# First layer of a two-layer kernel: the state gradient of the block three back right behind the state product, and VectorE's update and bias work put into another order

## The chip, the cores and the metric

The kernel runs on one core of a Trainium2 chip. The time is the device time of one execution in microseconds (us); the time of a kernel is the median of its runs.

## What is computed

Two layers act on x, four sequences of 512 tokens with 128 features. Each layer normalizes x and adds an attention part and an expert part to it. The change concerns the attention part of the first layer, a recurrence over chunks of 64 tokens for 16 heads of width 64, in which each head keeps a 64x64 state W and a bias b, updated by a gradient step for each chunk:

```python
def step(carry, inp):
    W, bb = carry
    xq_c, xk_c, xv_c = inp
    lr = jax.nn.sigmoid(jnp.einsum('bhkc,hcd->bhkd', xk_c, theta) + tb)
    eta = token_eta * (BASE_LR * lr / HD)
    Z1 = xk_c @ W + bb
    mu = Z1.mean(-1, keepdims=True)
    std = jnp.sqrt(Z1.var(-1, keepdims=True) + EPS)
    x_hat = (Z1 - mu) / std
    y = g * x_hat + be
    grad_output = y - (xv_c - xk_c)
    gxh = grad_output * g
    grad_x = (HD * gxh - gxh.sum(-1, keepdims=True) - x_hat * (gxh * x_hat).sum(-1, keepdims=True)) / (HD * std)
    dW = jnp.einsum('bhkc,bhkd->bhcd', eta * xk_c, grad_x)
    db = (eta * grad_x).sum(-2, keepdims=True)
    Wn, bn = (W - dW, bb - db)
    Zq = xq_c @ Wn + bn
    ...
    out = xq_c + g * ((Zq - mu2) / std2) + be
    return ((Wn, bn), out)
```

The first layer's expert part (16 experts that each take 32 tokens of a sequence), the second layer's attention and its four rounds of a mixture of four experts follow; the change does not touch them.

## The kernel before, in words

Each engine has a program of its own, written out by hand, and the programs meet through semaphores. There is no scheduler: the order of the calls in the source is the order in which an engine works, and an engine that waits holds up all that stands behind it.

The recurrence has 8 chunks (NC). A chunk is cut into four blocks, two halves of the heads (hf) by two pairs of sequences (g), so that there are 32 blocks. The loop `for s in range(4 * NC + 6)` stands in the programs of TensorE (PE), VectorE (DVE) and ScalarE (ACT), and one to 4 * NC in that of GpSimd (POOL). Step s does the gradient side of block s and the query side of block s - 4, which reads the state after the update by that block. Below, the class of a step is s mod 4.

A step runs through the engines as follows, with the names of the helpers and the lines of the profile.

- PE: `XK_` turns the keys (L1336). `bias_rows` puts the bias into the two banks of Z (L1283); at an even s it waits for `bias_split`, and always for `xhat` and `normed` of the step before, which still read those banks. `state_q` and `state` multiply queries and keys by the state (L1292); both wait for `state_updated`, the update by block s - 4. `target` (L1324, then L1238 to L1240) multiplies the tokens by the weights of the target. In odd steps `bias` sums the rated gradients of two blocks into the bias bank (L1357). `queries` and `keys` make the features of a coming chunk (L1238 to L1240). `att` multiplies the normed and turned output by the output weights in steps of class 0 and 1 (L1400). `dW` is the state gradient, 16 matmuls of 64x64 (L1372). `turn` turns the normed output of the step before (L1389).
- ACT: squares of Z (`squares`, L485, and `squares_q`, L521), a copy of the target out of its bank (`take_u`, L495), in odd steps the rounded part of the bias (`bias_high`, L516), then the deviation (`deviation`, L490), the copy of the queries (L510) and `deviation_q` (L526).
- DVE: `centre` of the block before (L830), the two sums of squares (L792, L854), the reciprocal (L798), `xhat` (L804), `rdev_q` (L859), in odd steps `bias_low` (L842), which writes the rest of the bias into `Bhl` and gives `bias_split`, `normed` (L864), `rate_of` (L811), `gradient` (L818), `update` (L849), `sum_gx` (L824) and `sum_gx_xhat` (L836).
- POOL: `scaled` (L1149), between `xhat` and `gradient`; `gx_xhat` (L1155), `rated` of the block before (L1175), which `bias` and `dW` wait for, `part` (L1161) and `less` (L1168).

The waits of the operations that move are these: dW(s) waits for the rated gradient of block s, for the turned keys of it, and for update(s - 1), since the blocks share the banks of dW; update(s) waits for dW(s).

```python
r = slice(32 * (s % 4), 32 * (s % 4) + 4)          # in bias_rows
if s >= 4:
    pe.wait_ge(CHUNK["bias_split"], s // 2 - 1)
if s:
    pe.wait_ge(CHUNK["xhat_ready"], min(s, 4 * NC))
if s > 4:
    pe.wait_ge(CHUNK["normed_ready"], s - 4)
```

Of the kernel before, what the change touches and what calls it, by code (L numbers as in the profile page):

```python
# [63 lines left out]
def build(nc, A, out, const_d, dbg=None):  # L64
    with ExitStack() as ctx:
# [625 lines left out]
        def _(dve):  # L691
# [75 lines left out]
            def without_eight(k):  # L767
                link(dve.match_replace(wrk[:, :], m8[:, k, :], lgt[:, :] if k == 0 else wrk[:, :], -3.0e38))
# [37 lines left out]
            def rate_of(s):  # L806
                if s in LIVE:
                    u = s % 4
                    hf, g = u // 2, u % 2
                    dve.wait_ge(CHUNK["z_rdev"], s + 1)  # L810
                    dve.tensor_tensor(sm[:, u, 3, :], eta[:, s // 4, g, 8 * hf:8 * hf + 8], sm[:, u, 2, :], ALU.mult).then_inc(CHUNK["rate_ready"], 1)  # L811
# [44 lines left out]
            def rdev_q(s):  # L856
                if s in AFTER:
                    dve.wait_ge(CHUNK["zq_dev"], s - 3)
                    dve.reciprocal(rq[:, s % 4, 2, :], rq[:, s % 4, 1, :]).then_inc(CHUNK["zq_rdev"], 1)  # L859

            def normed(s):
                if s in AFTER:
                    dve.wait_ge(CHUNK["zq_rdev"], s - 3)
                    dve.tensor_tensor(by_pair(Am[:, s % 2, :]), zq_of, per_pair(rq[:, s % 4, 2, :]), ALU.mult).then_inc(CHUNK["normed_ready"], 1)  # L864
# [17 lines left out]
            for s in range(4 * NC + 6):  # L882
                if s != 2:
                    centre(s - 1)
                sum_squares(s), sum_squares_q(s)
                if s == 1:
                    without_eight(0)
                rdev(s), xhat(s)
                if s == 0:
                    rates_scaled(), router_logits()  # L890
                elif s == 1:
                    best_eight(1)
                elif s == 2:
                    best_eight(3)
                elif s == 3:
                    without_eight(3)
                elif s == 4:
                    chosen()
                elif s == 5:
                    ranks_in_order()  # L900
                elif s == 6:
                    ranks_of_chosen()
                rdev_q(s)
                if s % 2:
                    bias_low((s - 3) // 2)
                normed(s), rate_of(s - 1), gradient(s), update(s - 2), sum_gx(s)
                if s == 0:
                    best_eight(0)
                elif s == 1:
                    without_eight(1)  # L910
                elif s == 3:
                    dve.memset(wones[:, :], 1.0)
                elif s == 6:
                    router_weights()
                sum_gx_xhat(s)
                if s == 1:
                    centre(1), best_eight(2), without_eight(2)
                if s == 8:
                    dve.wait_ge(moe_loaded, 16 * N_M)
                    for j in range(4):  # L920
                        r = slice(32 * j, 32 * j + 32)
                        dve.tensor_copy(b3s[r, :], eb[r, 2, :].rearrange("p (g j) -> p j g", j=4)[:, j, :])
                if s == 4 * NC:
                    dve.wait_ge(CHUNK["xk_ready"], 4 * NC)
                    onehot(0, range(2))
                elif s == 4 * NC + 1:
                    onehot(0, range(2, NT))
                elif s == 4 * NC + 2:
                    weighted(0, range(3))
                elif s == 4 * NC + 3:  # L930
                    weighted(0, range(3, NT))
# [296 lines left out]
        def _(pe):  # L1228
# [200 lines left out]
            for s in range(4 * NC + 6):  # L1429
                if s == 4 * NC + 2:  # L1430
                    pe.wait_ge(CHUNK["keys_taken"], 4 * NC)
                    pe.wait_ge(CHUNK["gx_ready"], 4 * NC)
                    gather(0, range(2))
                elif s == 4 * NC + 4:
                    gather(0, range(2, NT))
                XK_(s), bias_rows(s), state_q(s), state(s), target(s)
                if s % 2:
                    bias((s - 3) // 2)
                if s == RANKS:
                    pe.wait_ge(ranks_ready, 2)  # L1440
                    pe.wait_ge(out_weights_taken, 2)
                    pe.wait_ge(CHUNK["turned_taken"], RANKS - 5)
                    for k in range(2):
                        for t in range(NT):
                            last = pe.transpose(misc[:, (k * NT + t) * BE:(k * NT + t + 1) * BE], rkp[:, k, t * P:(t + 1) * P], ident[0:BE, 0:BE])
                    last.then_inc(ranks_turned, 1)
                queries(s)
                if s == 4 * NC + 5:
                    pe.wait_ge(CHUNK["state_updated"], 4 * NC)
                    turn_weights(0, 1)  # L1450
                att(s - 2), keys(s), dW(s - 2)
                if s == 4 * NC + 5:
                    turn_weights(0, 2), turn_weights(0, 3)
                if s == 4 * NC + 4:
                    pe.wait_ge(CHUNK["queries_taken"], 4 * NC)
                    turn_weights(0, 0)
                turn(s - 1)
                if s == 0:
                    pe.wait_ge(CHUNK["u_taken"], 1)
                    features(first_bank, 2, 0, wkh, wkl).then_inc(CHUNK["keys_ready"], 1)  # L1460
                if s == 1:
                    pe.wait_ge(CHUNK["xk_taken"], 2)
                    features(second_bank, 3, 0, wkh, wkl).then_inc(CHUNK["keys_ready"], 1)
                    pe.wait_ge(choice_step, 1)
                    pe.wait_ge(wq_loaded, 16)
                    for a in range(NP):
                        last = pe.transpose(bank[a // 4][:, a % 4 * P:(a % 4 + 1) * P], wq[:, a * P:(a + 1) * P], ident)
                    last.then_inc(wq_turned, 1)
                if s == 3:
                    pe.wait_ge(wo_loaded, 16 * 5)  # L1470
                    pe.wait_ge(wq_turned_taken, 2)
                    pe.wait_ge(rates_biased, 1)
                    for a in range(NP):
                        pe.matmul(misc[:, 0:P], wqT[:, a, :], wo[:, a, :], start=(a == 0), stop=(a == NP - 1))
                    for a in range(NP):
                        last = pe.matmul(misc[:, P:P + 1], wo[:, a, :], bet[:, a:a + 1], start=(a == 0), stop=(a == NP - 1))
                    last.then_inc(out_weights, 1)
# [265 lines left out]
```

## Time and profile before

| | |
|---|---|
| runs | 940.82, 939.50, 935.36 us; median 939.5 |
| profiled execution | 940.72 us, its span 938.9 us |
| mean granted clock of TensorE | 0.98 of full speed |
| busy in the span | PE 94%, DVE 83%, ACT 60%, POOL 68% |
| the loop of the recurrence | about 31 to 320 us of the span |
| the chain that ended last | PE 58%, DVE 23%, issue 11%, POOL 4%, ACT 3% |

The page lists the busy time of each engine and the chain of waits followed back from the end. A timeline lists an engine's instructions with their starts; where one starts before its forerunner ends, the two overlap in the engine's pipeline, and the distance of their starts is what the first one costs. PEclk is the granted clock of TensorE as a share of its full 2.4 GHz.

### The profile page before, as it was taken

Reading aid. Unit: us, or ns where it says so; the run is one execution under the profiler, and the core shown is the slowest. Engines: PE = TensorE matmul, PEld = TensorE weight load, DVE = VectorE, ACT = ScalarE, POOL = GpSimd, SP = SyncE. Lnnn points to the kernel's source line nnn. Section 1 sums busy time; section 2 is a strip of 40 time slices with the busy share of each in tenths; the row PEclk is TensorE's granted clock in tenths of the full one; section 3 lists DMA queues with packets and bytes.
Section 4 is the critical chain, followed back from the end, with each engine's and each line's share of the span. In section 5 each row is a group of like instructions: output and inputs, shape, how many; then the busy total and the mean of one; then the engine's idle time right before and its main releaser. Section 6 shows DMA issues by size and latency. Waiting matters only on the chain.

```text
span 938.9 us, 19758 instructions
## 1 busy us (share of the span) xinstructions
PE 880.9 (94%) x7768; PEld 608.6 (65%) x7768; DVE 778.0 (83%) x1180; ACT 560.0 (60%) x845; POOL 638.9 (68%) x582
## 2 busy tenths in 40 slices
PE   2888999999998899999999999999999999999997
PEld 2556777877776788655666665666665665665664
DVE  7888998899886648788888888888888888878876
ACT  4446666666653464655766655766656666666663
POOL 5377788888886050956955966955966965866863
PEclk9789999999998899999999999999999999999999
DMA  8100000000000321120110220110220110120110
GB/s 229 33 2 2 2 3 2 2 2 3 2 3 1 95 86 32 49 66 7 61 57 24 65 78 10 57 60 24 63 77 14 53 63 23 60 78 20 46 50 25
DMA packets 24965, 38.27 MB, mean 41 GB/s; under 512 B 9317, under 2 KB 15481, under 8 KB 22825
## 3 DMA queue, kind: packets, MB, share of 16 engines
q1 hardware_dynamic: 23240, 34.74, 12.0%
q10 hardware_dynamic: 1632, 2.27, 0.8%
q8 instruction: 62, 1.02, 0.5%
q14 instruction: 31, 0.25, 0.1%
HBM read 28.29 MB, written 1.43 MB: 32 GB/s over the span
## 4 chain that ended last, share of the span: by engine, by line
PE 58%; DVE 23%; issue 11%; POOL 4%; ACT 3%; DMA 1%; SPq 0%; POOLq 0%; DVEq 0%
PE bank L1238 12%; PE bank L1240 10%; PE bank L1239 10%; DVE hdh L1032 6%; PE bank L1400 3%; PE bank L1544 3%; PE quad L1576 3%; DVE add L1041 3%; PE quad L1292 3%; DVE mx L1025 2%; PE quad L1283 2%; POOL arena L1149 2%; PE bank L1357 2%; PE quad L1372 1%; PE bank L1595 1%
## 5 line engine op out<-in xcount | busy, mean ns | idle before, releaser
L1025 DVE TENSOR_REDUCE mx<-quad 128x4 f32<-128x2048 f32 x64 | 146.4, 2287 | 37.5 <-PE quad L1576 37.4
L1206 POOL CAST hdh<-xn 128x512 fp32r<-128x512 f32 x96 | 66.3, 690 | 155.0 <-ACT xn L660 155.0
L677 ACT ACTIVATE ex<-quad 128x2048 f32<-128x2048 f32 x64 | 120.6, 1885 | 59.0 <-PE quad L1586 59.0
L1208 POOL TENSOR_TENSOR hdl<-hd,hdh 128x512 fp32r<-128x512 f32 x96 | 129.8, 1352 | 7.7
L1208 POOL TENSOR_TENSOR hdl<-xn,hdh 128x512 fp32r<-128x512 f32 x96 | 128.9, 1342 | 7.7
L1238 PE MATMUL bank<-hdh,W2h 128*128 128x512 f32 x256 | 113.7, 444 | 6.1 <-DVE hdl L1035 4.9
L660 ACT ACTIVATE xn<-bank,b1c 128x512 f32<-128x512 f32 x128 | 88.0, 687 | 26.9 <-POOL hdl L1208 18.4
L660 ACT ACTIVATE hd<-bank,b1c 128x512 f32<-128x512 f32 x112 | 77.0, 688 | 44.7 <-PE bank L1240 28.4
L1240 PE MATMUL bank<-hdl,W2h 128*128 128x512 f32 x256 | 101.1, 395 | 0.0
L1239 PE MATMUL bank<-hdh,W2l 128*128 128x512 f32 x256 | 101.0, 395 | 0.0
L1238 PE MATMUL bank<-cH,W1h 128*128 128x512 f32 x192 | 80.9, 422 | 0.7 <-DVE cL L1052 0.7
L1238 PEld LDWEIGHTS bank<-hdh,W2h 128*128 128x128 f32 x256 | 47.9, 187 | 45.4 <-DVE hdl L1035 14.8
L1240 PE MATMUL bank<-cL,W1h 128*128 128x512 f32 x192 | 76.0, 396 | 0.0
L1239 PE MATMUL bank<-cH,W1l 128*128 128x512 f32 x192 | 75.9, 395 | 0.0
L1206 POOL CAST hdh<-hd 128x512 fp32r<-128x512 f32 x96 | 71.8, 748 | 0.0
L1544 PE MATMUL bank<-ex,Vx 128*32 128x512 f32 x512 | 65.1, 602 | 0.0
L1149 POOL TENSOR_TENSOR arena<-arena,gg 128x512 f32<-128x512 f32 x32 | 42.5, 1329 | 29.5 <-DVE arena L804 29.5
L1047 DVE TENSOR_TENSOR cur<-cur,add 128x512 f32<-128x512 f32 x60 | 59.8, 997 | 2.1
L1155 POOL TENSOR_TENSOR arena<-arena 128x512 f32<-128x512 f32 x32 | 41.0, 1280 | 27.5 <-DVE arena L818 27.5
L1240 PEld LDWEIGHTS bank<-hdl,W2h 128*128 128x128 f32 x256 | 48.1, 188 | 11.5
L1041 DVE SCALAR_TENSOR_TENSOR add<-bank,b2T,cwB 128x512 f32<-128x512 f32 x64 | 47.5, 743 | 8.9 <-PE bank L1240 8.9
L1239 PEld LDWEIGHTS bank<-hdh,W2l 128*128 128x128 f32 x256 | 48.3, 189 | 5.9
(315 smaller groups left out, 2197.7 us busy)
## 6 DMA issues: line engine op xcount, KB each, us to landing
cwB<-gate_rows SPq DMA_DIRECT2D x16, 1024.0 KB, 4.6
kx<-kqh SPq DMA_DIRECT2D x32, 64.0 KB, 2.1
qx<-kqh SPq DMA_DIRECT2D x32, 64.0 KB, 2.1
W1r<-in_L_ffn_W SPq DMA_DIRECT2D x1, 1024.0 KB, 10.2
kx<-kql SPq DMA_DIRECT2D x16, 64.0 KB, 2.1
qx<-kql SPq DMA_DIRECT2D x16, 64.0 KB, 2.1
rec<-rec_rows SPq DMA_DIRECT2D x32, 32.0 KB, 2.1
out<-fin SPq DMA_DIRECT2D x4, 256.0 KB, 2.3
```

The lines of the kernel that those rows point to most:

```text
L660: act.activation(tile(n), bank[TILE_BANK[n % 3]][:, :], ACT.Gelu_apprx_tanh, bias=b1c[:, n:n + 1]).then_inc(ROUND["gelu_ready"], 1)
L677: act.activation(ex[:, t % 2, :, :], quad[:, :, :], ACT.Exp, scale=float(AD) ** -0.5).then_inc(ROUND["exps_ready"], 1)
L1025: dve.tensor_reduce(mx[:, t, :, 0], quad[:, :, :], AX_X, ALU.max, negate=True).then_inc(ROUND["score_max"], 1)
L1041: dve.scalar_tensor_tensor(out=add[:, e % 2, :], in0=bank[6 if e % 2 else 4][:, :], scalar=b2T[:, e:e + 1], in1=cwB[:, e, :], op0=ALU.add, ...
L1047: dve.tensor_tensor(now, before, add[:, e % 2, :], ALU.add).then_inc(ROUND["cur_added"], 1)
L1149: pool.tensor_tensor(t1[:, u, :], xh[:, u, :], gg[:, 512 * hf:512 * hf + 512], ALU.mult).then_inc(CHUNK["scaled_ready"], 1)
L1206: pool.tensor_copy(hdh[:, m % RING, :], tile(n)).then_inc(ROUND["pool_split"], 1)
L1208: pool.tensor_tensor(hdl[:, m % RING, :], tile(n), hdh[:, m % RING, :], ALU.subtract).then_inc(ROUND["pool_split"], 1)
L1238: pe.matmul(to, lh, rh, start=start, stop=False, skip_group_check=True)
L1239: pe.matmul(to, ll, rh, start=False, stop=False, skip_group_check=True)
L1240: return pe.matmul(to, lh, rl, start=False, stop=stop, skip_group_check=True)
L1544: last = pe.matmul(bank[5][32 * h:32 * h + 32, :], Vx[:, t, QH * r + h, :], ex[:, t % 2, h, :], start=(t == 0), stop=(t == NT - 1), skip_g ...
```

## The change

Two calls move on each of two engines. On PE, the state gradient is called with the block three back instead of two back, and stands right behind the state product, ahead of the target. On DVE, `update` is called for the block three back as well and stands right behind `normed`, ahead of `rate_of`, `gradient` and `sum_gx`; `bias_low`, which stood ahead of `normed`, now stands behind `sum_gx`.

```diff
@@ -900,10 +900,9 @@
                     ranks_in_order()
                 elif s == 6:
                     ranks_of_chosen()
-                rdev_q(s)
+                rdev_q(s), normed(s), update(s - 3), rate_of(s - 1), gradient(s), sum_gx(s)
                 if s % 2:
                     bias_low((s - 3) // 2)
-                normed(s), rate_of(s - 1), gradient(s), update(s - 2), sum_gx(s)
                 if s == 0:
                     best_eight(0)
                 elif s == 1:
@@ -1433,7 +1432,7 @@
                     gather(0, range(2))
                 elif s == 4 * NC + 4:
                     gather(0, range(2, NT))
-                XK_(s), bias_rows(s), state_q(s), state(s), target(s)
+                XK_(s), bias_rows(s), state_q(s), state(s), dW(s - 3), target(s)
                 if s % 2:
                     bias((s - 3) // 2)
                 if s == RANKS:
@@ -1448,7 +1447,7 @@
                 if s == 4 * NC + 5:
                     pe.wait_ge(CHUNK["state_updated"], 4 * NC)
                     turn_weights(0, 1)
-                att(s - 2), keys(s), dW(s - 2)
+                att(s - 2), keys(s)
                 if s == 4 * NC + 5:
                     turn_weights(0, 2), turn_weights(0, 3)
                 if s == 4 * NC + 4:
```

The lines behind the first hunk stand one higher in the changed kernel (L1371 for dW instead of L1372).

The order of VectorE in an odd step of the loop, from the reciprocal of the deviation on (`arena` holds most tiles of the layer, `Bhl` the split bias, `Wst` the state), before:

```order
L798 RECIPROCAL sm<-sm 128x8
L804 TENSOR_TENSOR arena<-quad,sm 128x512
L859 RECIPROCAL rq<-rq 128x8
L842 SCALAR_TENSOR_TENSOR Bhl<-Bhl,cst,bank 36x512
L864 TENSOR_TENSOR arena<-quad,rq 128x512
L811 TENSOR_TENSOR sm<-eta,sm 128x8
L818 TENSOR_TENSOR arena<-arena 128x512
L849 TENSOR_TENSOR Wst<-Wst,quad 128x2x256
L824 TENSOR_REDUCE sm<-arena 128x8
L836 TENSOR_REDUCE sm<-arena 128x8
```

and with the change:

```order
L798 RECIPROCAL sm<-sm 128x8
L804 TENSOR_TENSOR arena<-quad,sm 128x512
L859 RECIPROCAL rq<-rq 128x8
L864 TENSOR_TENSOR arena<-quad,rq 128x512
L849 TENSOR_TENSOR Wst<-Wst,quad 128x2x256
L811 TENSOR_TENSOR sm<-eta,sm 128x8
L818 TENSOR_TENSOR arena<-arena 128x512
L824 TENSOR_REDUCE sm<-arena 128x8
L842 SCALAR_TENSOR_TENSOR Bhl<-Bhl,cst,bank 36x512
L836 TENSOR_REDUCE sm<-arena 128x8
```

The write of `Bhl` (`bias_low`) has gone from ahead of `normed` (L864) to behind the sum of the gradient (L824), and the update (L849) from behind the gradient (L818) to ahead of it.

The order of PE from the opening of a step of class 3 to the query features, before:

```order
L1283 MATMUL quad<-Bhl,pair 128x512 x2
L1292 MATMUL quad<-Wst,arena 64x64 x32
L1324 MATMUL bank<-gbr,ones 128x512
L1238 MATMUL bank<-wuh,xth 128x512
L1239 MATMUL bank<-wuh,xtl 128x512
L1240 MATMUL bank<-wul,xth 128x512
L1357 MATMUL bank<-arena,cst 32x512 x2
```

and with the change:

```order
L1282 MATMUL quad<-Bhl,pair 128x512 x2
L1291 MATMUL quad<-Wst,arena 64x64 x32
L1371 MATMUL quad<-arena 64x64 x16
L1323 MATMUL bank<-gbr,ones 128x512
L1237 MATMUL bank<-wuh,xth 128x512
L1238 MATMUL bank<-wuh,xtl 128x512
L1239 MATMUL bank<-wul,xth 128x512
L1356 MATMUL bank<-arena,cst 32x512 x2
```

The sixteen matmuls of dW (L1372 before, L1371 now) stand between the state product and the target, where none stood.

## Rows read from the trace of the kernel before

**Rows 1.** The page, busy time of each engine in the whole span.
```profile
PE 880.9 (94%) x7768; PEld 608.6 (65%) x7768; DVE 778.0 (83%) x1180; ACT 560.0 (60%) x845; POOL 638.9 (68%) x582
```

**Rows 2.** Timeline of PE: start us, duration us, engine, line, operation, tiles, shapes, count.
```profile
150.95 0.39 PE L1240 MATMUL bank<-wul,xth 128*128 128x512 f32 x1
...
154.58 0.73 PE L1283 MATMUL quad<-Bhl,pair 4*128 4x512 f32 x2
...
157.14 0.40 PE L1240 MATMUL bank<-wul,xth 128*128 128x512 f32 x1
157.64 1.05 PE L1357 MATMUL bank<-arena,cst 128*32 128x512 f32 x4
...
162.01 0.70 PE L1283 MATMUL quad<-Bhl,pair 4*128 4x512 f32 x2
...
165.48 1.95 PE L1400 MATMUL bank<-arena,wog 128*128 128x128 f32 x16
...
169.95 0.73 PE L1283 MATMUL quad<-Bhl,pair 4*128 4x512 f32 x2
...
179.10 0.73 PE L1283 MATMUL quad<-Bhl,pair 4*128 4x512 f32 x2
...
185.28 0.73 PE L1283 MATMUL quad<-Bhl,pair 4*128 4x512 f32 x2
...
287.18 3.09 PE L1400 MATMUL bank<-arena,wog 128*128 128x128 f32 x16
```

**Rows 3.** The chain that ended last, in order of time: the piece of one dW.
```profile
160.31 0.62 PE quad L1372 x32
```

**Rows 4.** Timeline of ACT in steps of class 2 and 3.
```profile
151.38 0.60 ACT L495 ACTIVATE arena<-bank 128x512 f32<-128x512 f32 x1
151.88 0.29 ACT L490 ACTIVATE sm<-sm,cst 128x8 f32<-128x8 f32 x1
...
158.74 0.59 ACT L516 ACTIVATE Bhl<-bank 36x512 fp32r<-36x512 f32 x1 [0.57 <-PE bank L1357]
159.23 0.29 ACT L490 ACTIVATE sm<-sm,cst 128x8 f32<-128x8 f32 x1
```

**Rows 5.** Timeline of DVE in a step of class 3, and one gradient of class 1.
```profile
159.79 0.69 DVE L804 TENSOR_TENSOR arena<-quad,sm 128x512 f32<-128x512 f32 x1
...
160.57 0.69 DVE L842 SCALAR_TENSOR_TENSOR Bhl<-Bhl,cst,bank 36x512 fp32r<-36x512 f32 x1
161.19 0.67 DVE L864 TENSOR_TENSOR arena<-quad,rq 128x512 f32<-128x512 f32 x1
...
161.87 0.69 DVE L818 TENSOR_TENSOR arena<-arena 128x512 f32<-128x512 f32 x1
162.48 0.68 DVE L849 TENSOR_TENSOR Wst<-Wst,quad 128x512 f32<-128x512 f32 x1
163.08 0.68 DVE L824 TENSOR_REDUCE sm<-arena 128x8 f32<-128x512 f32 x1
...
177.43 0.68 DVE L818 TENSOR_TENSOR arena<-arena 128x512 f32<-128x512 f32 x1
```

**Rows 6.** Timeline of POOL: the product between xhat and gradient, class 1.
```profile
175.90 1.28 POOL L1149 TENSOR_TENSOR arena<-arena,gg 128x512 f32<-128x512 f32 x1 [1.03 <-DVE arena L804]
```

**Rows 7.** Timelines of DVE and PE around the opening of step 6.
```profile
84.91 0.69 DVE L818 TENSOR_TENSOR arena<-arena 128x512 f32<-128x512 f32 x1
...
85.07 0.70 PE L1283 MATMUL quad<-Bhl,pair 4*128 4x512 f32 x2 [1.69 <-DVE arena L864]
```

**Rows 8.** Windows: stretch, length, busy PE PEld DVE ACT POOL, granted PE clock, DMA.
```profile
83.40:85.00 1.60, 0.00 (x0) 0.00 (x0) 1.54 (x5) 1.12 (x3) 0.84 (x1) 1.00 0.00 0
...
283.50:284.50 1.00, 0.00 (x0) 0.00 (x0) 1.00 (x3) 0.60 (x1) 0.99 (x1) 1.00 0.00 0
...
286.50:289.50 3.00, 3.00 (x16) 3.00 (x15) 2.49 (x5) 1.05 (x3) 2.92 (x4) 0.50 0.00 0
...
298.20:299.70 1.50, 0.00 (x0) 0.00 (x0) 1.32 (x3) 0.53 (x1) 0.00 (x0) 1.00 0.00 0
```

## The prediction

> **What bounds the kernel now.** I read the page first: TensorE (PE) is busy 94% of a span of 938.9 us, VectorE 83%, GpSimd (POOL) 68% [rows 1]. The change touches only the step loop of the first layer, roughly 30 to 320 us, so I read that stretch alone. Its steps repeat every four (one chunk of tokens): the bias matmuls that open a step of class 3 (class is s mod 4) start at 154.58 and again at 185.28 us, so a chunk takes 30.7 us; the openings between them are 162.01 (class 0), 169.95 (class 1) and 179.10 (class 2) [rows 2]. PE has almost no holes: between the target's last matmul at 157.14 and the bias sums at 157.64 it loses 0.27 us (0.23 is the spacing of such matmuls), and before 162.01 about 0.12, because VectorE's `normed` of class 3 only ends at 161.19 + 0.67 = 161.86 [rows 2, 5]. What the reader should see is that last pair: 0.15 us after VectorE's operation ends, PE opens class 0. **PE is the bound by its work, but twice in a chunk VectorE arrives just in time.** Those are the places where an order can cost something.
>
> `bias_rows(s+1)` at an even s+1 waits for three things: `xhat`, `normed(s)` and `bias_split`, which `bias_low` of odd step s gives. Today `bias_low` stands ahead of `normed` (160.57, then 161.19 [rows 5]), so `normed` is the one that ends last.
>
> **The change, part by part.** Nothing is added or taken away: 32 state gradients (`dW`) and 32 updates remain, and no DMA moves. Every term is therefore a move.
>
> *1. dW(s-3) stands behind the state product, ahead of the target.* One dW takes 0.62 us of PE [rows 3]. PE has the same work per step, so by itself this is worth nothing. But the target product now ends 0.62 us later, and on ScalarE the copy of the target (`take_u`, L495) stands ahead of the deviation (L490). In class 2 the copy started at 151.38, right behind the target (150.95 + 0.39 = 151.34), and the deviation at 151.88, as soon as the copy let it [rows 2, 4]. So the deviation moves to 152.50, and with it `xhat`, POOL's product, the gradient, and POOL's rated gradient of the step before, for which PE's bias sums wait: 157.64 becomes 158.26. These release `bias_high` on ScalarE (158.74), behind which the class 3 deviation stands (159.23) [rows 4]; `xhat` of class 3 goes from 159.79 [rows 5] to 160.41. The two delays are one chain and count once: 0.62.
>
> *2. update(s-3) stands behind `normed`.* It needs about 0.6 us of VectorE (162.48 to 163.08 [rows 5]), in a stretch in which VectorE waits for POOL in class 2, and in class 3 it takes exactly the place of `bias_low` (160.57 to 161.19 is 0.62 as well). Its dW is issued over 3 us ahead. The gradient is still released by POOL. Cost nothing; the cover is POOL's 1.28 us product [rows 6], and if it were gone the gradient would be 0.6 later. `state(s)` now needs an update of the step before rather than of two steps before, but that ends before `bias_low` does, so it is never the last wait.
>
> *3. `bias_low` stands behind `sum_gx`.* This is the expensive one. Class 3: gradient at 161.87 + 0.62 = 162.49, `sum_gx` 0.61 later at 163.10, `bias_low` 0.60 later at 163.70 and 0.72 long, to 164.42 (durations from rows 5), PE 0.15 later at 164.57. It opened at 162.01: **plus 2.56 us**. Queued behind that opening are the whole state product and everything PE does in class 0, a step with two output products in which PE has no slack of its own to give back. Class 1: POOL starts its product at 175.90 and needs 1.28 [rows 6]; 0.62 later it ends at 177.80, the gradient starts at 177.85 instead of 177.43 [rows 5], `bias_low` at 179.06, its end at 179.80, PE at 179.95 instead of 179.10: **plus 0.85**. Class 0 and class 2 in between are paced by PE and need no new wait: 0.17 us of the 0.62 shows in front of class 3's opening, but the chain of part 1 runs beside it.
>
> *Sum over the loop.* One chunk gives 2.56 + 0.85 = 3.4 us. From the opening of step 8 to that of step 32 lie six chunks: 20.5. Steps 0 to 8 are different, since VectorE also has the routing work there: at step 6 the gradient goes from 84.91 to 85.35 and the opening from 85.07 [rows 7] to 85.35 + 0.61 + 0.60 + 0.74 + 0.15 = 87.45, plus 2.4; at step 8 the second move costs 1.9 again, of which I let VectorE, late anyway, absorb 0.3: plus 1.6. Against that the first dW falls due one step later, and PE's 0.62 in front of the output weights of step 3 goes away. Together 3.4. Behind step 32 no gradient stands between the operations; I put 0.3 for `bias_low` behind the update at step 33. Sum: **24.2 us**.
>
> *4. The clock.* The trace of before does not show waits of PE as long as the new ones: 0.12 + 2.56 = 2.7 us in front of each class 0. The nearest rows are the PE holes of the loop, all with no matmul in them. Behind the holes at 283.5 (1.0 us of it in the row) and 298.2 (1.5) the granted clock fell from 1.00 to 0.50, that is from 2.4 to 1.2 GHz (286.5 to 289.5 shows 0.50); behind the one at 83.4 (1.6) it was still 1.00 a moment later [rows 8] and the page shows no dip there. Two falls of three at some half of the length; I take it that a 2.7 us hole brings the clock down nearly every time. The price of one fall: in such a stretch the sixteen output matmuls took 3.09 us instead of 1.95 [rows 2], 1.1 more, and the query matmuls ahead of them some 0.4; part of the low stretch can lie within the hole itself, where it costs nothing. Bounds 0 and 1.5, and I take 1.2. Eight holes of 2 us and more (steps 6, 8, 12 ... 32): **9.6 us**.
>
> The Trainium skill speaks against this term. "TensorE: Matmul & The Clock Gate", section "HAM oscillation — how this bites in real kernels", lets the clock drop only for idle gaps longer than any that I compute here. By that rule the sum is 24.2 alone, about 964. The falls behind the holes of 1.0 and 1.5 us in rows 8 disagree with it, so the rows decide, and the page stays as a rival.
>
> *Sum.* 24.2 + 9.6 = 33.8 us. The profiled execution took 940.7 us (span 938.9), so 974.5; the median of the three runs is 939.5, 1.2 us below, hence **973 us**.
>
> **The rivals.**
> - *The clock stays up.* All of the above without part 4: 939.5 + 24.2 = 964. For it: the hole at 83.4 did no harm, and PE is busier around the new holes than around 283 or 298. Against it: the new holes are longer than all of those. Chance 0.20.
> - *The target copy holds nobody up.* If ScalarE's copy is ready in time after all, 0.62 falls away in class 3 and 0.4 in class 1: 2.4 us a chunk, some 17 in all, 957 without falls of the clock. Against it: L490 started when L495 let it go [rows 4]. Chance 0.08.
> - *Faster, and this is the other side: VectorE's order costs nothing, and PE keeps running.* `normed` ends 0.62 earlier in odd steps, which would remove the 0.12 in front of class 0, and dW ahead of the bias sums would cover the 0.27 there: 0.4 us a chunk, 3 in all, 936. It decides as soon as `bias_low` ends before 161.86, the point at which `normed` ended. By rows 5 even the gradient in front of it only starts then. Chance 0.04.
> - *Nothing moves in the time.* `bias_low` is late, but PE recovers it in later steps: about 940. It would take 3.4 us of slack in each chunk; I count 0.4. Chance 0.04.
>
> The forecast, with the clock falling behind most of the eight holes, has the rest, 0.64.
>
> **How the numbers follow.** About 0.5% (4.7 us) is what a measurement of this kernel can tell from no change. The forecast and the first two rivals are slower by more than that: 0.64 + 0.20 + 0.08 = 0.92. Same 0.04, faster 0.04. The forecast's own bounds are 964 (falls that cost nothing) and, with twice 1.2 for each of the eight, 983; POOL products that run beside VectorE work could add 3. That gives 986 at the top. At the bottom the range takes in both slower rivals, 957, and leaves the last two out.
>
> **What would show it.** Right: the chunk grows from 30.7 to about 34 us, 35 with a fall; PE's largest waits in the loop become those of the bias matmuls (L1283 before, L1282 now) for VectorE's `Bhl` operation (L842), about 2.7 us eight times and 0.9 us seven times; L842 starts about 1.2 us behind the gradient; in class 2 the deviation on ScalarE starts 0.62 us later against the opening of its step (151.88 against 148.4 before); behind 320 us all is as before, shifted. The clock term is right if the windows behind the long holes show 0.50 for about 3 us. Wrong: if the bias matmuls still wait for `normed` (L864), the move of `bias_low` was misread; if it waits for `bias_low` but under 2 us, part 1 is too large; if PEclk stays at 1.00, the first rival holds.

## The result: 4% slower, and the profile after

The changed kernel takes 977.7 us (median of 4 runs, 977.5 to 979.04), the kernel before 937.6 beside it (4 runs, 935.36 to 940.82); in later rounds it stood at 939 to 940. The ratio is 1.041, 95% interval 1.039 to 1.044: slower, 5 us above the forecast of 973 and inside the range. The profiled execution took 977.8 us; its page begins with

```profile
span 976.0 us, 19758 instructions
...
PE 891.5 (91%) x7768; PEld 617.5 (63%) x7768; DVE 772.1 (79%) x1180; ACT 559.3 (57%) x845; POOL 638.0 (65%) x582
```

against [rows 1]. The count of instructions is the same. PE's matmuls are "busy" for 10.6 us more, which is not more work but the same work at half the clock in some stretches; VectorE's busy time fell by 5.9 us (why, stands at the end).

The timeline of PE in one chunk, cut to the openings of its steps (columns as in [rows 2], in brackets the idle time before the instruction and who ended it):

```profile
223.03 0.73 PE L1282 MATMUL quad<-Bhl,pair 4*128 4x512 f32 x2
...
233.03 0.73 PE L1282 MATMUL quad<-Bhl,pair 4*128 4x512 f32 x2 [0.62 <-DVE Bhl L842]
...
239.21 0.69 PE L1282 MATMUL quad<-Bhl,pair 4*128 4x512 f32 x2 [0.23 <-DVE arena L864]
...
249.19 0.79 PE L1282 MATMUL quad<-Bhl,pair 4*128 4x512 f32 x1 [2.42 <-DVE Bhl L842]
```

These are classes 1, 2, 3 and 0. In [rows 2] none of them has a wait in brackets. PE's waits from 100 to 340 us, by what it waited for (us in total, times, longest):

```profile
PE quad L1282 <- DVE Bhl L842: 22.3, 13, 4.0
PE bank L1335 <- ACT arena L464: 2.9, 12, 0.3
PE quad L1282 <- DVE arena L864: 1.8, 6, 0.6
```

So PE now stands 22 us for VectorE's write of `Bhl`: six times 2.43, six times 0.62, and 4.04 in front of step 32. In [rows 5] the two operations `L842` and `L864` stood in the other order. VectorE in the step of class 3:

```profile
244.91 0.69 DVE L804 TENSOR_TENSOR arena<-quad,sm 128x512 f32<-128x512 f32 x1
245.57 0.20 DVE L859 RECIPROCAL rq<-rq 128x8 f32<-128x8 f32 x1
245.80 0.69 DVE L864 TENSOR_TENSOR arena<-quad,rq 128x512 f32<-128x512 f32 x1
246.41 0.68 DVE L849 TENSOR_TENSOR Wst<-Wst,quad 128x512 f32<-128x512 f32 x1
247.00 0.16 DVE L811 TENSOR_TENSOR sm<-eta,sm 128x8 f32<-128x8 f32 x1
247.08 0.69 DVE L818 TENSOR_TENSOR arena<-arena 128x512 f32<-128x512 f32 x1
247.80 0.69 DVE L824 TENSOR_REDUCE sm<-arena 128x8 f32<-128x512 f32 x1
248.40 0.73 DVE L842 SCALAR_TENSOR_TENSOR Bhl<-Bhl,cst,bank 36x512 fp32r<-36x512 f32 x1
```

L842 ends at 249.13 and PE opens at 249.19. The lengths of the steps, from opening to opening, once the loop is steady (us; for 0 to 1 the value of steps with the clock up):

| class | before | after | why |
|---|---|---|---|
| 2 to 3 | 6.18 | 6.18 | |
| 3 to 0 | 7.41 | 9.97 | +2.56, `Bhl` |
| 0 to 1 | 7.93 | 7.68 | -0.25, not foreseen |
| 1 to 2 | 9.14 | 10.00 | +0.86, `Bhl` |
| chunk | 30.66 | 33.83 | +3.17 |

A hole below is a stretch in which PE stands still, a fall one in which its granted clock is 0.50, half of the full one. Behind the long holes the clock falls in most cases. Windows of after (columns as in [rows 8], the granted clock is the third number from the end):

```profile
109.50:111.50 2.00, 2.00 (x98) 1.63 (x98) 1.39 (x2) 0.19 (x1) 2.00 (x2) 1.00 0.00 0
143.30:145.30 2.00, 2.00 (x37) 1.35 (x40) 1.40 (x2) 0.00 (x0) 2.00 (x2) 0.50 0.00 0
...
181.00:183.00 2.00, 2.00 (x88) 2.00 (x84) 0.23 (x1) 0.31 (x1) 1.92 (x2) 0.50 0.00 0
215.40:217.40 2.00, 2.00 (x95) 1.64 (x98) 1.42 (x2) 0.17 (x1) 2.00 (x2) 1.00 0.00 0
...
249.20:251.20 2.00, 2.00 (x34) 1.35 (x38) 1.46 (x2) 0.00 (x0) 2.00 (x2) 0.50 0.00 0
```

The five follow holes of the same kind (2.42 or 2.43 us) in front of steps 8, 12, 16, 20 and 24: three times 0.50, twice 1.00. Of the eight long holes six had a fall behind them (6, 12, 16, 24, 28, 32). A fall costs 1.5 us (16, 28: 9.15 and 9.17 instead of 7.68) or 2.6 to 2.7 (12, 24: 10.38 and 10.31).

**Where the 37.1 us between the two spans went:** 1.6 in front of the first opening, 7.2 in steps 0 to 8, 27.5 in steps 8 to 32 (183.99 became 211.53), under 0.1 in steps 32 to 35, 0.8 behind. Of the 27.5, six chunks of 3.17 are 19.0, the four falls at steps 12, 16, 24 and 28 are 8.3, and 0.3 are a longer step 19 (10.26 us instead of 9.97, see experiment 1). The 1.6 in front is no effect of the change that can be told from chance: the first opening lay at 30.5 in the profile before, and at 28.9 and 32.1 in those of the first two experiments, which change nothing ahead of it (28.6 to 32.1 in all twelve profiles).

### The profile page after: what moved, and what is told of

Read it like the earlier page. It is cut to its first block, busy times and chain, and to the rows that moved or that the text cites. A ratio compares the mean times of both kernels' runs of the same rounds, so it can differ in the third digit from the quotient of the medians.

```text
span 976.0 us, 19758 instructions
## 1 busy us (share of the span) xinstructions
PE 891.5 (91%) x7768; PEld 617.5 (63%) x7768; DVE 772.1 (79%) x1180; ACT 559.3 (57%) x845; POOL 638.0 (65%) x582
## 4 chain that ended last, share of the span: by engine, by line
PE 57%; DVE 24%; issue 11%; ACT 4%; POOL 3%; DMA 1%; SPq 0%; DVEq 0%; POOLq 0%
PE bank L1237 11%; PE bank L1239 9%; PE bank L1238 9%; DVE hdh L1031 6%; PE quad L1291 3%; PE bank L1543 3%; PE quad L1575 3%; DVE add L1040 2%; PE quad L1282 2%; DVE mx L1024 2%; PE bank L1356 2%; PE bank L1399 2%; DVE arena L804 2%; PE quad L1371 1%; POOL arena L1148 1%
## 5 line engine op out<-in xcount | busy, mean ns | idle before, releaser
L660 ACT ACTIVATE hd<-bank,b1c 128x512 f32<-128x512 f32 x112 | 77.0, 688 | 44.8 <-PE bank L1239 28.6
L1282 PE MATMUL quad<-Bhl,pair 4*128 4x512 f32 x72 | 29.4, 491 | 32.1 <-DVE Bhl L842 26.2
```

The costliest lines, as they stand in the source:

```text
L660: act.activation(tile(n), bank[TILE_BANK[n % 3]][:, :], ACT.Gelu_apprx_tanh, bias=b1c[:, n:n + 1]).then_inc(ROUND["gelu_ready"], 1)
```

## The experiments

**Theory A:** `bias_low` behind `sum_gx` makes the holes, the holes bring the clock down, and dW ahead of the target adds a little through ScalarE. **Rivals:** (B) the early dW and the early update cost as much by themselves; (C) the holes alone make the time, and the clock is a by-product.

### 1. `bias_low` back ahead of `normed`, the rest of the change kept

```diff
-rdev_q(s), normed(s), update(s - 3), rate_of(s - 1), gradient(s), sum_gx(s)
+rdev_q(s)
 if s % 2:
     bias_low((s - 3) // 2)
+normed(s), update(s - 3), rate_of(s - 1), gradient(s), sum_gx(s)
```

> The changed kernel with bias_low put back ahead of normed; dW and update stay where the change put them. Main theory (bias_low's place is what costs, dW ahead of the target adds 0.6 us to the chain in front of it): the distance of the openings of class 3 and class 0 falls from 9.97 to about 8.0 us (7.41 in the kernel before), that of class 1 and class 2 from 10.0 to 9.1, and no fall of the clock stands behind steps 8 to 28; in all 938 to 945 us. Rival (dW behind the state product, or the update ahead of the gradient, is what costs): both distances stay above 9.3, and the time above 955.

945.1 us, ratio 1.007 (1.004 to 1.009). Steps 6.18, 7.91, 7.65, 9.31: a chunk of 31.05, only 0.39 above before. The opening of class 0 in it:

```profile
229.26 0.46 PE L1283 MATMUL quad<-Bhl,pair 4*128 4x512 f32 x1 [0.36 <-DVE arena L864]
```

The time is at the upper edge of what was expected (938 to 945), and no fall stands behind steps 8 to 28. Some 33 of the 38 us (977.7 less 945.1) go with `bias_low`'s place. That is theory A; of B 5 us are left. The profile puts 2.3 of them in six chunks (class 0 still opens 0.5 later) and 2.7 in steps 0 to 8, but it is of the longest of the six executions, 949.9 us, so it holds more than the 5. Two of its steps are left aside in the lengths above, 19 (9.46 us) and 20 (8.87): PE stood in the middle of dW, and the profile names nobody for whom it waited ("issue"):

```profile
189.16 0.64 PE L1372 MATMUL quad<-arena 64*64 64x64 f32 x29
191.25 0.33 PE L1372 MATMUL quad<-arena 64*64 64x64 f32 x3 [1.45 <-issue]
```

The same stood in dW in step 20 (0.92 us), in steps 19 and 20 of experiment 5 (1.06 and 0.90), in step 16 of experiment 4 (1.42) and for 0.19 us in step 19 of after. These are the four kernels with dW right behind the state product; none of the other eight profiles has such a stop in dW from step 4 on. So it looks like a second, small cost of that place. Its cause stays open, and it was not tried by itself.

### 2. Only `bias_low` behind `sum_gx`, dW and update at their old places

```diff
-rdev_q(s)
-if s % 2:
-    bias_low((s - 3) // 2)
-normed(s), rate_of(s - 1), gradient(s), update(s - 2), sum_gx(s)
+rdev_q(s), normed(s), rate_of(s - 1), gradient(s), update(s - 2), sum_gx(s)
+if s % 2:
+    bias_low((s - 3) // 2)
```

> The kernel before with one move alone: bias_low behind sum_gx; dW(s-2) and update(s-2) stay as before. Here the update stands between the gradient and bias_low, so bias_low starts 1.8 us behind the gradient (1.25 in the changed kernel), but nothing delays the copy of the target. Main theory: class 3 to class 0 about 9.9 us, class 1 to class 2 about 10.0, holes of about 2.5 and 0.9 us in front of them, some falls of the clock; in all 968 to 980 us, so this one move costs as much as the whole change. Rival (the moves of dW carry the cost): within 5 us of the kernel before.

984.0 us, ratio 1.046 (1.042 to 1.050): outside what was expected, and slower than the whole change. Two things were missed. In class 1 the update, here between the gradient and `bias_low`, waits for a dW that PE gives late:

```profile
235.71 0.69 DVE L818 TENSOR_TENSOR arena<-arena 128x512 f32<-128x512 f32 x1
236.71 0.69 DVE L849 TENSOR_TENSOR Wst<-Wst,quad 128x512 f32<-128x512 f32 x1 [0.31 <-PE quad L1371]
237.32 0.68 DVE L824 TENSOR_REDUCE sm<-arena 128x8 f32<-128x512 f32 x1
238.03 0.75 DVE L842 SCALAR_TENSOR_TENSOR Bhl<-Bhl,cst,bank 36x512 fp32r<-36x512 f32 x1
```

which makes the hole in front of class 2 1.17 us instead of 0.62. And the clock fell behind every hole in front of steps 8 to 28, mostly for long (class 0 to 1 took 10.8 to 11.0 us in the first five, 9.4 in the last). Run 10 asks whether the second is indeed the clock. Moving dW and the update earlier thus softens what `bias_low`'s move does: they are the cheap part of the change, and in its company a useful one.

### 3. dW behind the target and the bias sums

```diff
-XK_(s), bias_rows(s), state_q(s), state(s), dW(s - 3), target(s)
+XK_(s), bias_rows(s), state_q(s), state(s), target(s)
 if s % 2:
     bias((s - 3) // 2)
+dW(s - 3)
```

> The changed kernel with dW(s-3) behind the target and, in odd steps, behind the bias sums instead of ahead of both. Main theory (0.62 us of each hole comes from dW in front of the target copy): class 3 to class 0 falls from 9.97 to 9.35 us, class 1 to class 2 from 10.0 to 9.4, the hole in front of class 0 from 2.43 to 1.8; 6 chunks times 1.2 makes 7 us, and falls of the clock get rarer: 962 to 971 us. Rival (the copy of the target is not on the path, the deviation waits for something else): class 3 to class 0 stays within 0.1 of 9.97.

984.4 us, ratio 1.048 (1.045 to 1.050): the expectation failed. Class 3 to 0 is 10.60, not 9.35, though `xhat` of class 2 did come earlier (4.04 us behind its opening, 4.51 in after); that of class 3 did not (5.70 in both). VectorE in class 3:

```profile
209.14 0.69 DVE L804 TENSOR_TENSOR arena<-quad,sm 128x512 f32<-128x512 f32 x1
210.43 0.20 DVE L859 RECIPROCAL rq<-rq 128x8 f32<-128x8 f32 x1 [0.59 <-ACT rq L526]
210.66 0.69 DVE L864 TENSOR_TENSOR arena<-quad,rq 128x512 f32<-128x512 f32 x1
```

dW now stands in front of the query features; ScalarE's `deviation_q` (L526) is queued behind its copy of those (L510), and `rdev_q`, `normed`, update, gradient and `bias_low` stand behind it on VectorE. The early dW delays the target copy by half a microsecond, the later one delays the query copy by 0.6 (it starts 6.16 us behind the opening of class 3, 5.54 in after). Between state product and target is the better of the two places.

### 4. The long holes filled

The changed kernel, with matmuls whose results are not read put into PE's wait for the split bias in front of steps 6, 8, 12 to 32.

```diff
+for _ in range({6: 11, 32: 10}.get(s, 9 if s % 4 == 0 and 8 <= s < 32 else 0)):
+    pe.matmul(quad[:, 2, :], wkh[:, 0:P], xth[:, 0:512], start=True, stop=True, skip_group_check=True)
 if s >= 4:
     pe.wait_ge(CHUNK["bias_split"], s // 2 - 1)
```

> The changed kernel with extra matmuls whose result bias_rows overwrites, in the hole in front of bias_rows of steps 6, 8, 12 to 32: between the wait for normed and the wait for bias_split, 9 to 11 of 512 columns (about 2.1 to 2.5 us), so that PE works there but should not open later than before. They compute nothing that is used. Main theory (the holes bring the clock down, at 1.5 to 2.7 us each): the openings of class 0 and 1 stand 7.7 us apart in every chunk instead of 7.7 to 10.4, the clock stays at 1.00 behind those openings, and the time falls by 7 to 12 us, to 965 to 971. Rival (the clock falls for another reason, such as the small matmuls in and around the opening): the falls stay and the time is 977 or more.

964.8 us, ratio 1.027 (1.025 to 1.030): 13 us below the changed kernel with 75 matmuls more. The hole of class 0 and windows at the places where after showed 0.50:

```profile
207.94 2.33 PE L1278 MATMUL quad<-xth,wkh 128*128 128x512 f32 x9
210.49 0.73 PE L1284 MATMUL quad<-Bhl,pair 4*128 4x512 f32 x2 [0.21 <-DVE Bhl L842]
```

```profile
143.00:146.00 3.00, 3.00 (x36) 2.75 (x28) 2.04 (x4) 2.40 (x6) 1.63 (x2) 1.00 0.00 0
180.00:184.00 4.00, 4.00 (x37) 3.99 (x37) 3.05 (x8) 2.40 (x7) 1.32 (x2) 1.00 0.00 0
...
249.00:256.00 7.00, 7.00 (x134) 5.50 (x132) 6.14 (x11) 3.95 (x9) 5.41 (x5) 1.00 0.01 4
```

The opening of class 0 comes no earlier (9.97 and 10.03), so only the clock differs. What after lost by falls that this run does not have: 8.3 in steps 12 to 28, 2.3 at step 6 (9.02 against 6.73), 2.6 at step 32 (8.46 against 5.84), together 13.2. The spans of the two profiles differ by less, 10.6: in this one PE also stops for 1.42 us in dW of step 16 (16 to 17 took 9.43 us with the clock up), and a fall that comes later, from 326.7 us on, eats some of the gain at step 32. The median of the runs, 13 us lower, is the better measure. Rival C is out.

### 5. The deviation ahead of the target copy

Experiment 1, and on ScalarE `deviation` in front of `take_u` and `bias_high`.

```diff
-take_u(s)
+deviation(s), take_u(s)
...
-deviation(s)
```

> The kernel of e1 (bias_low ahead of normed, dW(s-3) behind the state product) and on ScalarE the deviation moved ahead of the copy of the target and of bias_high. e1 took 31.05 us a chunk against 30.66 before. Main theory (what is left of e1's loss is the deviation, held up by the copy of a target that dW pushed back): the hole of 0.23 us in front of class 3 and of 0.36 in front of class 0 go, and since dW between state product and target saves PE some 0.25 us in a step, the chunk falls to 30.1 to 30.4 us: 2 to 5 us faster than the kernel before. Rival (the deviation was not on the path, another wait is): the chunk stays at 31.0 and the time 4 to 6 us above before.

950.2 us, ratio 1.011 (1.009 to 1.012); experiment 1 had 1.007. Not faster but 0.3 us a chunk longer. `xhat` came earlier against the step, by 0.7 us in class 1 and 0.4 in class 3 (0.1 in class 2, nothing in class 0), and this was of no use:

```profile
176.79 0.69 DVE L803 TENSOR_TENSOR arena<-quad,sm 128x512 f32<-128x512 f32 x1
178.33 0.20 DVE L858 RECIPROCAL rq<-rq 128x8 f32<-128x8 f32 x1 [0.85 <-ACT rq L526]
178.56 0.75 DVE L841 SCALAR_TENSOR_TENSOR Bhl<-Bhl,cst,bank 36x512 fp32r<-36x512 f32 x1
```

The query's deviation is queued behind everything on ScalarE and did not move, so VectorE waits for it instead. With `bias_low`, `normed` and the update in front of the gradient, the gradient then starts at 180.63 us although POOL's product ended at 178.95.

### 6. Routing work behind the sum of the gradient, steps 4 to 6 (kernel before)

```diff
+rdev_q(s)
+if s % 2:
+    bias_low((s - 3) // 2)
+normed(s), rate_of(s - 1), gradient(s), update(s - 2), sum_gx(s)
 if s == 4:
...
-rdev_q(s)
-if s % 2:
-    bias_low((s - 3) // 2)
-normed(s), rate_of(s - 1), gradient(s), update(s - 2), sum_gx(s)
```

> The kernel before with VectorE's three routing operations of steps 4, 5 and 6 (0.7, 1.2 and 0.9 us, between xhat and normed) behind sum_gx instead. PE waits 0.61, 1.69 and 1.01 us for normed in front of steps 5, 6 and 7. If those waits are real losses, the opening of step 8 comes 1.5 to 3 us earlier against that of step 4 (31.2 us before) and the kernel gains as much. Rival: POOL's chain is as late and takes their place, gain under 0.5 us. Not part of the change: it asks whether VectorE's order in front of an opening is worth something in the other direction too.

939.1 us, ratio 0.999 (0.997 to 1.000): no difference. This kernel's ranks of the chosen experts are made from other numbers, since `normed` overwrites a tile that they read. PE's wait of 1.7 us in front of step 6 [rows 7] shrank to 0.44, but steps 4 to 8 took 30.96 instead of 31.21: PE's bias sums came 0.7 us later, by POOL's chain. The rival was right.

### 7 and 9. Holes of the kernel before filled

```diff
+if s == 4 * NC:
+    pe.wait_ge(CHUNK["u_taken"], 4 * NC)
+    fill(first_bank, 4)
+elif s == 4 * NC + 2:
+    fill(first_bank, 6)
+elif s == 4 * NC + 3:
+    pe.wait_ge(CHUNK["queries_taken"], 4 * NC)
+    fill(second_bank, 7)
```

> The kernel before with extra matmuls (4, 6 and 7 of 512 columns, results unused, in banks that lie free) in PE's holes in front of steps 32, 34 and 35. Main theory (a hole brings the clock down): no granted clock of 0.50 between 286 and 314 us, where the kernel before shows 0.50 for 3 and 13 us; 2 to 6 us faster. Rival (the falls cost nothing there, PE waits for others anyway, or come back all the same): within 1 us of the kernel before.

936.9 us, ratio 0.996 (0.995 to 0.998), 2.8 us below the kernel before and at the low end of what was expected. From step 32 to 35 the loop takes 19.59 us instead of 22.23, and the stretch at half the clock in [rows 8] is gone:

```profile
283.00:303.50 20.50, 18.66 (x250) 13.82 (x249) 15.56 (x25) 6.90 (x15) 12.43 (x10) 1.00 0.01 2
```

That the clock stays up there without the extra matmuls happens too: the profile of experiment 6, whose steps 32 to 35 are those of the kernel before, took 19.50 us for them, in an execution of 934.8 us, its shortest of twelve. So the two profiles alone show little, and the gain rests on the medians of 9 and 20 runs.

Run 9 adds five such matmuls in front of the first target, where PE stood from 31.8 to 34.3 us.

> The kernel before with the filler matmuls in front of steps 32, 34 and 35 (as in e7), and five more in target(0) ahead of its waits, where PE stood still from 31.8 to 34.3 us before. Theory (the low clock follows the hole): the low stretch at 34 to 44 us goes, and the run is 1 to 4 us below the one with the tail filled alone, 933 to 936 us. Rival (the low clock there comes from the first layer's start, not from this hole, or VectorE bounds these steps): the same as the tail filled alone, 936 to 938 us. The filler results are not read.

935.6 us, ratio 0.996 (0.995 to 0.998), within the 933 to 936 of the theory, but not to be told from run 7. The windows of 33.8 to 44 us, first run 9, then run 7:

```profile
33.80:44.00 10.20, 6.63 (x66) 5.08 (x66) 8.17 (x11) 3.92 (x8) 4.87 (x3) 1.00 0.00 0
```

```profile
33.80:44.00 10.20, 9.51 (x64) 7.21 (x63) 7.38 (x11) 3.18 (x6) 5.47 (x4) 0.54 0.00 0
```

The clock is up all through, and PE is busy 2.9 us less for the same stretch. Much of that turns into waiting: ahead of step 2 PE stands 4.12 us for ScalarE's L464 instead of 0.90, and the clock falls there, at 44.8 us. Step 8 opens at 99.66 us in both profiles, but run 9's first opening lay 2.05 us later (31.01 and 28.96), which is within the chance named above, so these two profiles do not tell whether nothing or 2 us are gained. The low clock of that stretch went once most of the hole was filled; whether that is worth anything in time stays open. These two kernels are the only ones below the kernel before with an interval that leaves out 1, by less than the 0.5% of the prediction.

### 8. The early update with dW at its old place

Experiment 1, with `dW(s - 3)` where `dW(s - 2)` stood before.

```diff
-XK_(s), bias_rows(s), state_q(s), state(s), dW(s - 3), target(s)
+XK_(s), bias_rows(s), state_q(s), state(s), target(s)
...
-att(s - 2), keys(s)
+att(s - 2), keys(s), dW(s - 3)
```

> The kernel of e1 with dW(s-3) where dW(s-2) stood, behind the keys: of the change only the update ahead of the gradient, and the block three back, are left. Main theory (that part costs nothing): the chunk is 30.66 us within 0.15, the hole in front of class 0 stays near 0.1, the time within 2 us of the kernel before. Rival (the update in front of the gradient lengthens the chain by 0.6 us): holes in front of class 3 and class 0, chunk of 31 or more.

945.9 us, ratio 1.006 (1.004 to 1.007), a chunk of 31.50 and not the expected 30.66. VectorE in class 1:

```profile
178.24 0.69 DVE L864 TENSOR_TENSOR arena<-quad,rq 128x512 f32<-128x512 f32 x1
179.70 0.69 DVE L849 TENSOR_TENSOR Wst<-Wst,quad 128x512 f32<-128x512 f32 x1 [0.76 <-PE quad L1372]
180.30 0.16 DVE L811 TENSOR_TENSOR sm<-eta,sm 128x8 f32<-128x8 f32 x1
180.38 0.69 DVE L818 TENSOR_TENSOR arena<-arena 128x512 f32<-128x512 f32 x1
```

The update waits for a dW at the end of PE's step, and the gradient is queued behind it; POOL then stands 2.46 us, and the next bias sums are late. The rival's "31 or more" came true, though by this wait for dW and not by the length of the update. The early update is free only with the early dW.

### 10. Experiment 2 with the long holes filled

The edit of experiment 4, put on the kernel of experiment 2.

> The kernel before with only bias_low moved behind sum_gx (as in e2), and 9 to 11 filler matmuls in PE's wait for the bias split in front of steps 6, 8, 12 to 32. Theory (e2 missed its forecast by the falls of the clock in every chunk): no clock of 0.50 between 95 and 320 us, step of class 0 to 1 7.9 us, 3 to 0 9.9 us, 1 to 2 at most 10.1 us, 964 to 968 us in all. Rival (e2 is long because bias_low behind sum_gx costs more by itself): the time stays at 975 us or more though the clock is up. The filler results are not read.

967.9 us, ratio 1.030 (1.028 to 1.033): 16 us below experiment 2, as expected for falls of the clock. The steps are 7.95, 10.47, 6.16 and 9.87, without a fall 34.45 a chunk. Class 1 to 2 was expected at 10.1 at most; the missing 0.4 is the waiting update. Two short falls remain that were not expected, behind two of the unfilled holes of 1.26 us in front of class 2. One of the holes, and a window behind it:

```profile
226.12 0.70 PE L1284 MATMUL quad<-Bhl,pair 4*128 4x512 f32 x2 [1.26 <-DVE Bhl L842]
```

```profile
229.00:230.00 1.00, 1.00 (x6) 0.90 (x5) 0.89 (x2) 0.50 (x2) 0.55 (x1) 0.50 0.00 0
```

## Why the prediction was right, point by point

**Part 1, dW ahead of the target (0.62 us of delay).** Right in its chain, a little too large. In after ScalarE's timeline of class 2 reads

```profile
236.49 0.60 ACT L495 ACTIVATE arena<-bank 128x512 f32<-128x512 f32 x1 [0.48 <-PE bank L1239]
236.98 0.29 ACT L490 ACTIVATE sm<-sm,cst 128x8 f32<-128x8 f32 x1
```

and the deviation starts 3.95 us behind the opening, before 3.48 (151.88 less 148.40): 0.47, not 0.62, and `xhat` of class 3 comes 5.70 behind its opening instead of 5.21. PE's rows say why: from the start of the state product to that of the target it was 1.09 us before (149.06 to 150.15), and it is 1.56 with dW in between (233.69 to 235.25). So dW adds 0.47 at this place; the 0.62 was its price at the end of a step. What failed is the sentence "PE has the same work per step, so by itself this is worth nothing". From class 0 to 1 a step got 0.25 us shorter. With dW at the end of the step it stayed at 7.92 to 7.97 (experiments 8 and 10), with dW behind the state product it is 7.64 to 7.68 in four kernels (after, 1, 4, 5), and behind the target it is 8.03 (experiment 3, where the clock was up). So the saving belongs to that place. From class 2 to 3 it went into a new wait of 0.23 us. The timelines show where PE is quicker (distances of starts, the step from 162.01 before and that from 215.35 in after): the state product takes 0.99 instead of 1.09, dW 0.57 instead of 0.63, the last key matmul 0.12 instead of 0.21, the turning 0.46 instead of 0.49. These lie where PE goes over between 64x64 and 128-wide matmuls, and with dW right behind the state product, which is 64x64 too, it does so one time less each way. That this is the reason fits, but was not tried.

**Part 2, the update ahead of the gradient (nothing).** Right: POOL's product of class 3 ended at 246.95 and the gradient started at 247.08. It held with a thin cover, and only in the company it had. With `bias_low` in front as well (experiments 1 and 5), the gradient is set by VectorE and no longer by POOL, by 0.85 us in class 1 of experiment 1 and 1.68 in experiment 5; with a late dW the cover is gone at once (experiment 8).

**Part 3, `bias_low` behind `sum_gx`.** The sum gave plus 2.56 and 0.85 us, measured 2.56 and 0.86. The first is partly chance: `xhat` came 0.13 earlier than assumed, and from its start to PE's opening it took 4.28 us and not 4.16. The chunk grew by 3.17 and not 3.4, by the 0.25 above. Six chunks: 19.0 for 20.5.

**Steps 0 to 8.** This is the term that was mis-sized: 3.4 plus one fall of 1.2 was the estimate, 7.2 was measured. At step 6 the hole was 3.87 us and the step into it 2.3 longer (estimated 2.4); step 7 lost 1.8 to the fall behind it, step 8 opened 2.4 later and not 1.6: VectorE did not absorb what I let it absorb. The step from 4 to 5 took 8.41 instead of 6.44, with the clock down. Against that steps 0 to 4 took 37.71 instead of 38.99, 1.3 less where 0.6 was estimated. The two falls make most of what the estimate missed: 2.3 for the one at step 6 (by experiment 4) and, as an estimate, 1.2 for the one at step 4 (the other 0.75 of that step is a longer wait in front of step 5, 1.36 instead of 0.61); without them 3.7 are left, close to the 3.4. The window of after in step 4, and the same stretch before:

```profile
69.80:75.00 5.20, 5.20 (x108) 4.38 (x108) 2.64 (x5) 1.96 (x4) 3.35 (x3) 0.67 0.02 3
```

```profile
69.50:75.00 5.50, 5.50 (x118) 4.49 (x118) 2.93 (x6) 4.06 (x10) 2.36 (x3) 1.00 0.01 3
```

No hole of part 3 is in front of it. The early update does not bring it: experiments 3 and 8 have that update and took 6.48 and 6.43, experiment 2 6.43. It is there in all four kernels with dW right behind the state product (after, 1 and 4 with 8.38 to 8.41, 5 with 7.59), but in run 9 too (7.56), where dW stands as before. What brings the clock down there stays open.

**Part 4, the clock (9.6).** Right in kind, larger in all: filling the holes gives back 13.0 us. The count was too high (six of eight) and the price too low: 1.5 for a short fall, 2.6 to 2.7 for a long one, against 1.2. The two errors partly cancel. The price came from the output matmuls in [rows 2]; it left out that the low stretch can outlast them. The rows also left out holes that the kernel before has in steps 0 to 8. The longest, 2.51 us from 31.83 to 34.34, had a fall of some 10 us; those from 49.91 to 51.82 and from 91.29 to 92.30 had none. The first was the nearest row to the new holes and speaks for the term, the others for the irregular answer that the last section shows. The rule of "TensorE: Matmul & The Clock Gate" of the Trainium skill (section "HAM oscillation — how this bites in real kernels"), by which only longer idle gaps than these bring the clock down, is not borne out here: four of the six falls stand behind holes of 2.4 us, and run 10 has two behind 1.26.

**The rivals.** "The clock stays up" would have given 964; with the holes filled the kernel took 964.8. That the two agree so closely is partly luck, since steps 0 to 8 are longer than computed and the filled kernel has no fall in front of its tail, where the kernel before has one. "The target copy holds nobody up" is refuted by the 0.47 us of part 1, "faster" and "nothing moves" by PE's 22.3 us of waits.

The sum by what was measured, against the span of before: 19.0 (chunks) + 8.3 (falls in them) + 0.3 (step 19) + 7.2 (steps 0 to 8, two falls included) + 0.8 (from step 32 on) + 1.6 (start) = 37.2 us (37.1 without the rounding of the terms); the prediction had 33.8. It came as close as that partly because the chunks were taken too long and the falls and steps 0 to 8 too cheap. For the 3 us by which the range went up for POOL's products beside VectorE's work the prediction named no row, and no such loss of time was found.

## What to carry to other kernels

Before an operation is moved back in a queue, ask who outside waits for it: 0.7 us of work that released a step of the nearly full engine was put behind five operations, and of the 2.6 us from the end of `normed` to its own end in class 3 2.4 came back as a hole of that engine. Moving an operation earlier is free only as long as what it waits for moves with it, and what stands behind it in the queue is released by somebody slower (experiment 8 breaks the first, 1 and 5 the second). Count with a hole of TensorE more than its length: here the clock took 13 of the 38 us, half as much again as the rest. Matmuls that compute nothing gave that back in experiments 4, 7 and 10; at the start of the loop (run 9) no gain in time can be told.

## What the runs showed of the hardware that was not expected

**The clock does not answer a hole in the same way each time.** Equal holes of 2.42 or 2.43 us in front of the same matmuls had a fall behind them four times in six in steps 8 to 28 (in two lengths); the same holes of 2.43 us in experiment 3 had one five times in six; holes of 2.5 to 2.6 us in experiment 2 had one every time, in front of the same six steps; two of the holes of 1.26 us in run 10 had one, the others none. In the fall at step 24 the clock went down within the hole (246.8 to 249.1 us shows 0.84), at step 16 only behind it (179.8 to 181.8 shows 0.58):

```profile
179.80:181.80 2.00, 2.00 (x46) 1.41 (x50) 1.43 (x2) 0.00 (x0) 2.00 (x2) 0.58 0.04 8
...
246.80:249.10 2.30, 0.00 (x0) 0.00 (x0) 2.27 (x5) 1.08 (x2) 1.40 (x3) 0.84 0.00 0
```

What decides between them stays open.

**A tiny VectorE operation can take as long as POOL's product beside it.** L811 multiplies 128x8 numbers. Groups of VectorE by line (count, busy us, mean ns), first before (100 to 283 us), then after (100 to 320 us):

```profile
L811 DVE TENSOR_TENSOR sm<-eta,sm 128x8 f32<-128x8 f32 x24 | 10.0, 419 | 0.0
```

```profile
L811 DVE TENSOR_TENSOR sm<-eta,sm 128x8 f32<-128x8 f32 x25 | 4.0, 159 | 0.0
```

Before, in an even step, it started behind `normed` while POOL's product ran, and lasted until that ended:

```profile
215.24 0.63 DVE L811 TENSOR_TENSOR sm<-eta,sm 128x8 f32<-128x8 f32 x1
215.88 0.69 DVE L818 TENSOR_TENSOR arena<-arena 128x512 f32<-128x512 f32 x1
```

Behind the update it starts when POOL is about done and takes 0.16. The long ones cost nothing in either kernel, since the gradient waits for the same product, but it accounts for the 5.9 us by which VectorE's busy time fell (0.26 us less in each of 24 instances is 6.2): less busy time, and no gain. VectorE is at 771 to 773 us in every run with the early update, which stands ahead of L811, and at 777 to 783 in all others. Operations that read a bank of PSUM on one side, such as L864 and L849 beside it, kept their 0.67 to 0.69 us. Why it lasts that long was not tested.
